# A vision tower on one core: the context from the normalised tokens times the keys, convolutions straight to tokens, a 128+64 split of 192 rows, and a new order on every engine

## The chip, the cores and the metric

The kernel runs on 1 core of one Trainium2 chip. Its time is the device time of one launch in microseconds (us). The kernel before takes 154.59 us, the median of 3 runs (153.43, 154.59, 155.02). Five engines work side by side, each through its own list of instructions in order: TensorE (PE in the rows; its weight loads are PEld), VectorE (DVE), ScalarE (ACT), GpSimd (POOL) and SyncE (SP), which issues the DMAs. They wait for each other by semaphores.

## What is computed

Two images of 32x128x128 are cut into 256 patches of 8x8 each. A convolution turns a patch into a token of 128 numbers. Two layers follow, then a head to 192 numbers per token, a linear attention and a feed-forward of 768 hidden units. Cut to what matters:

```
x = patches @ conv_w + conv_b
for each of 2 layers:
    y = ln(x) * g + b
    q, k, v = split(y @ qkv_w)                  # 8 heads of 64
    q = softmax(q, over a head's 64) * scale
    k = softmax(k, over the 256 tokens)
    x = x + (q @ (k^T v)) @ out_w + out_b
    x = x + gelu((ln(x)*g2+b2) @ ff1_w + ff1_b) @ ff2_w + ff2_b
h = ln(x) @ head_w + head_b                     # 192 wide
q, k, v = split(layernorm(h) @ W_qkv)           # 12 heads of 16
q, k = elu(q) + 1, elu(k) + 1
h = h + ((q @ (k^T v)) / (q . sum(k) + eps)) @ W_out + b_out
h = h + new_gelu(layernorm(h) @ W0 + b0) @ W1 + b1
```

## The kernel before

Everything is float32. A token tile is 128 tokens, so an image has two (`TILES`). Products that feed softmax or gelu are made from three products of reduced precision: operand a is split into `a_hi` (rounded) and `a_lo = a - a_hi`, and hi*hi, lo*hi and hi*lo are added in PSUM (`split_product`, L302, used by `weight_left` and `weight_right`). Those matmuls are one instruction each in the trace. A float32 matmul or product with plain operands shows as two MATMUL instructions.

**First stage.** SyncE issues all loads in one queue; `conv` (L320) adds 16 chunks of 128 channels-times-pixels for image 0 and 16 for image 1, with the convolution weight as the stationary operand and 256 tokens as the moving one. The result stands with the 128 features on the partitions, so ScalarE adds the bias (`embedding_bias`) and TensorE transposes it (L328) before VectorE can take the statistics of a token.

**Second stage, four steps.** A step `s` is one attention of one image: layer `s // 2`, image `s % 2`. The loop over `STEPS` sets the order on each engine: keys and queries of the step (`qkv_k`, `qkv_q`), values (`qkv_v`), transposed keys (`turn_k`, L379), `context` (L389: values times keys, eight 128x128 products of float32), `turn_q`, `context_out` (L398), `attend` (L413, which gives x after attention). Between them stands the feed-forward of the step before (`ff1`, `ff2`, L437) for the other image. In step 0 the place of the feed-forward is taken by the last 8 of the 16 chunks of image 1's convolution.

A layer norm (LN) is a chain over three engines: VectorE takes statistics (L645, L648) and adds epsilon (L650), GpSimd raises to the power -1/2 (`rsqrt`, tile `rstd`, L1103), VectorE subtracts and scales (`norm_apply`, tile `xn`, L655), TensorE transposes (L336), VectorE writes the high part with gain and offset (`norm_out_hi`, L662), ScalarE the exact value (L955), and VectorE or GpSimd their difference (`norm_out_lo`). GpSimd also makes the low parts of the weights (`weight_low_part`, L1157), adds bias rows, scales q, and multiplies the mixing masks into the last weights (`mix_fc` L1143, `mix_proj` L1150).

**Last stage.** After the fourth attention come, for each image, the remaining feed-forward, the last LN, `head`, LN3, `qkv3`, the linear attention, LN4, `fc3` and `proj3` (L561). The 192 rows of these products are cut in two chunks of 96, so a product takes 3 x 2 = 6 matmuls. Image 0's last products fill the gaps of image 1's attention. The raw weights of layer 1 and of the last products lie where `embed_sb` was, so their loads wait for the end of both convolutions.

## Time and profile before

| | |
|---|---|
| runs | 155.02, 154.59, 153.43 us; median 154.59 |
| profiled execution | span 154.1 us from its first to its last instruction; no other time is given for it |
| TensorE busy | 131.1 us, 85% |
| VectorE, ScalarE, GpSimd busy | 93.7, 66.0, 49.1 us |
| first key product | starts at 23.4 us |
| fourth attention added to x | at 95.3 us |
| last output instruction | starts at 151.25 us |

The profile is of one execution. Its span lies 0.5 us below the median of the three runs. The busy time of TensorE counts overlapping ends once; two matmuls of the same form that follow each other without a gap show their pace by the distance of their starts, or by the length of a group divided by its count.

### The profile page before, as it was taken

To read this page: it belongs to the slowest core of one execution; us is meant where nothing else is said; L and a number is where in the kernel's file an instruction comes from. 1 tells how busy PE (TensorE), PEld (TensorE's weight loads), DVE (VectorE), ACT (ScalarE), POOL (GpSimd) and SP (SyncE) were. 2 spreads that over 40 slices of the span, in tenths; PEclk is the share of its full clock that TensorE was granted. 3 is DMA by queue.
4 is the path that set the end of the run, shared out by engine and by line. 5 is a ranking of instruction groups with operands and counts; after the bars stand their busy time and mean duration, and the time that the engine had idled before them with its cause. 6 is when DMAs were issued, how large, how long until landed. Compare 5 with 4: busy or idle time off the path is not lost.

```text
span 154.1 us, 2173 instructions
## 1 busy us (share of the span) xinstructions
PE 131.1 (85%) x790; PEld 113.1 (73%) x790; DVE 93.7 (61%) x236; ACT 66.0 (43%) x149; POOL 49.1 (32%) x60
## 2 busy tenths in 40 slices
PE   1699889999779989799797996769987959999993
PEld 1468668797658968589576984559876948999992
DVE  1200087947799668977689757773957796145201
ACT  3010313906559746697375981144222040163230
POOL 0000020074162953447553673180671060004000
PEclk9999999999999999999999999956977995599999
DMA  5999997008800000000000000000000000000101
GB/s 161 285 421 415 421 412 262 0 4 265 209 0 0 6 0 0 0 0 4 0 0 0 0 4 0 0 0 2 2 0 0 4 0 0 0 4 0 51 0 51
DMA packets 3388, 11.50 MB, mean 75 GB/s; under 512 B 393, under 2 KB 1385, under 8 KB 3122
## 3 DMA queue, kind: packets, MB, share of 16 engines
q1 hardware_dynamic: 3378, 11.37, 20.6%
q8 instruction: 6, 0.10, 0.2%
q14 instruction: 4, 0.03, 0.1%
HBM read 10.98 MB, written 0.39 MB: 74 GB/s over the span
## 4 chain that ended last, share of the span: by engine, by line
PE 55%; DVE 26%; issue 5%; POOL 5%; ACT 3%; DMA 3%; SPq 0%; DVEq 0%; ACTq 0%; POOLq 0%
PE bank L302 16%; DVE xn L655 10%; PE bank L320 10%; PE bank L437 5%; PE bank L389 5%; PE bank L561 5%; POOL rstd L1103 3%; DMA embed_sb<-in_embed 3%; DVE stats L645 2%; DVE yT_hi L662 2%; DVE nkmax L695 2%; POOL yT_lo L1109 1%; PE bank L336 1%; PE bank L531 1%; PE bank L339 1%
## 5 line engine op out<-in xcount | busy, mean ns | idle before, releaser
L1103 POOL TENSOR_TENSOR rstd<-var,minus_half 128x2 f32<-128x2 f32 x14 | 10.2, 726 | 69.8 <-DVE var L650 69.8
L655 DVE TENSOR_SCALAR xn<-x,mv,rstd 128x128 f32<-128x128 f32 x20 | 13.8, 732 | 4.2 <-POOL rstd L1103 4.2
L320 PE MATMUL bank<-embed_sb 128*128 128x256 f32 x32 | 12.0, 544 | 4.4 <-DMA embed_sb<-in_embed 4.4
L955 ACT ACTIVATE yT<-bank,small_sb 128x256 f32<-128x256 f32 x10 | 5.7, 565 | 19.5 <-DVE yT_hi L662 16.4
L320 PEld LDWEIGHTS bank<-embed_sb 128*128 128x128 f32 x32 | 8.5, 277 | 7.2 <-DMA embed_sb<-in_embed 5.1
L1122 POOL TENSOR_TENSOR qn<-q,rqsum 128x512 f32<-128x512 f32 x8 | 8.2, 1044 | 15.2 <-DVE rqsum L719 15.2
L336 PE MATMUL bank<-small_sb,xn 128*128 128x128 f32 x20 | 4.4, 301 | 7.6 <-DVE xn L655 7.6
L413 PE MATMUL bank<-cw,qT 128*128 128x128 f32 x64 | 10.0, 289 | 0.4
L413 PEld LDWEIGHTS bank<-cw,qT 128*128 128x128 f32 x64 | 8.2, 190 | 2.0 <-issue 1.3
L336 PEld LDWEIGHTS bank<-small_sb,xn 128*128 128x128 f32 x20 | 2.0, 141 | 10.3 <-DVE xn L655 10.3
L975 ACT ACTIVATE kexp<-bank,nkmax 128x256 f32<-128x256 f32 x16 | 7.4, 473 | 4.3 <-DVE nkmax L695 4.3
L437 PE MATMUL bank<-restw,hid 128*128 128x128 f32 x64 | 9.1, 302 | 0.0
L437 PEld LDWEIGHTS bank<-restw,hid 128*128 128x128 f32 x64 | 8.8, 219 | 0.0
L389 PE MATMUL bank<-ktok,vtok 128*128 128x128 f32 x64 | 8.0, 278 | 0.4
L689 DVE COPY x<-bank 128x256 f32<-128x256 f32 x2 | 0.8, 420 | 12.3 <-PE bank L328 12.3
L561 PE MATMUL bank<-projw_raw,patches_sb 128*128 128x192 f32 x48 | 8.3, 326 | 0.0
L389 PEld LDWEIGHTS bank<-ktok,vtok 128*128 128x128 f32 x64 | 7.5, 192 | 1.0 <-issue 0.9
L655 DVE TENSOR_SCALAR xn<-h,mv,rstd 128x192 f32<-128x192 f32 x8 | 6.5, 859 | 2.2 <-POOL rstd L1103 2.2
L561 PEld LDWEIGHTS bank<-projw_raw,patches_sb 128*128 128x128 f32 x48 | 7.7, 190 | 0.0
L320 PE MATMUL bank<-patches_sb,embed_sb 128*128 128x256 f32 x32 | 7.6, 379 | 0.0
L302 PE MATMUL bank<-qkvw_hi,yT_hi 128*128 128x512 f32 x16 | 6.8, 427 | 0.8 <-DVE yT_hi L662 0.8
L1007 ACT ACTIVATE hid<-bank,small_sb 128x256 f32<-128x256 f32 x16 | 6.4, 474 | 2.0 <-PE bank L302 1.9
(142 smaller groups left out, 349.1 us busy)
## 6 DMA issues: line engine op xcount, KB each, us to landing
embed_sb<-in_embed SPq DMA_DIRECT2D x3, 768.0 KB, 7.9
patches_sb<-in_patches SPq DMA_DIRECT2D x2, 1024.0 KB, 12.1
restw<-in_rest_w SPq DMA_DIRECT2D x2, 768.0 KB, 16.1
qkvw<-in_qkv_w SPq DMA_DIRECT2D x3, 256.0 KB, 11.0
embed_sb<-in_qkv_w SPq DMA_DIRECT2D x1, 768.0 KB, 4.7
embed_sb<-in_embed SPq DMA_DIRECT2D x1, 576.0 KB, 4.4
projw_raw<-in_proj_w SPq DMA_DIRECT2D x1, 576.0 KB, 16.2
embed_sb<-in_fc_w SPq DMA_DIRECT2D x1, 576.0 KB, 7.6
```

The costliest lines, as they stand in the source:

```text
L302: mm = nc.tensor.matmul(dst, left(a, n), right(b, n), start=(k == 0 and n == 0), stop=(last and n == chunks - 1))
L320: mm = nc.tensor.matmul(dst[:, 0:TOKENS], embed_sb[:, c, 0:D], rhs, start=(c == 0), stop=(c == KCONV - 1))
L336: mm = nc.tensor.transpose(dst[:, t * P:(t + 1) * P], xn[i][:, t, 0:D], ident)
L389: mm = nc.tensor.matmul(VB[0][:, p * P:(p + 1) * P], vtok[i][:, t, p * P:(p + 1) * P], ktok[i][:, t, p * P:(p + 1) * P], start=(t == 0), s ...
L413: mm = nc.tensor.matmul(VB[0][:, t * D:(t + 1) * D], qT[i][:, t, c * P:(c + 1) * P], cw[i][:, c, :], start=(c == 0), stop=(c == PAIRS - 1))
L437: mm = nc.tensor.matmul(banks[t][:, 0:D], hid[i][:, c, t * P:(t + 1) * P], ff2w(l, c), start=(c == 0), stop=(c == FC - 1))
L561: mm = nc.tensor.matmul(QB[t][:, 0:E], hid3[i][:, c, t * P:(t + 1) * P], projw[:, c, :], start=(c == 0), stop=(c == HC - 1))
L655: last = nc.vector.tensor_scalar(xn[i][:, t, 0:width], src[:, t, 0:width], mv[i][:, t, 0:1], rstd[i][:, t:t + 1], ALU.subtract, ALU.mult)
L975: nc.scalar.activation(kexp[i][:, c, :], KB[c // 2][:, (c % 2) * TOKENS:(c % 2 + 1) * TOKENS], ACT.Exp, bias=nkmax[i][:, c:c + 1], accum_o ...
L1007: nc.scalar.activation(hid[i][:, c, :], src[:, (c % 2) * TOKENS:(c % 2 + 1) * TOKENS], ACT.Gelu, bias=col("ff1_b", l * FC + c)).then_inc(h ...
L1103: nc.gpsimd.tensor_tensor(rstd[i][:], var[i][:], minus_half[:], ALU.pow).then_inc(rstd_ready[i], 1)
L1122: nc.gpsimd.tensor_tensor(qn[i][:, t, :].rearrange("p (h d) -> p h d", h=HEADS), q[i][:, t, :].rearrange("p (h d) -> p h d", h=HEADS), rqs ...
```

## The change

Five things are changed at once.

1. **Context without v.** `qkv_v` and its two evictions are gone. The context k^T v = (k^T y) W_v is made from `keys_of_y`: two float32 products of 512 columns (y of a token tile against the keys of that tile), one eviction `ykey` in two halves (VectorE, then ScalarE), and four 128x128 products with the raw value weights. For that y must stand with tokens on the partitions, so LN1 is finished there: VectorE's `centre_and_gain` (x minus mean, times gain row) and `scale_and_offset` (times 1/deviation, plus offset row) replace `norm_apply`; after the transpose ScalarE copies the high part and VectorE subtracts it for the low part. Gain and offset rows come by two new broadcast loads. Epsilon is folded into the statistics, so L650 is gone.
2. **Token convolutions.** The token tile is stationary and the convolution weight moves: two products of 128 columns per chunk in place of one of 256, the bias as one more product (`conv_bias`), and no transposes. `warm_up` products of constants (8 calls) stand ahead of and between the first chunks.
3. **128+64 rows.** The 192 rows are cut into 128 and 64. High and low part of the 64 stand in one operand of 128 rows (`yT3_rest`), so a product takes 5 matmuls instead of 6.
4. **The last attention** multiplies q by the masked context first (`numerators3`, 102 columns per half: 96 of context and 6 of key sums), divides, then transposes and multiplies by the output weight. The product with ones over the tokens is gone.
5. **Order.** The loops are gone. Each engine's list is written out instruction by instruction, with PSUM banks given step by step; the weights no longer share memory with `embed_sb`, so no load waits.

```diff
         def _(sp):
-            half = KCONV // 2
-            for j in range(CONV_PIECES):
-                at = slice(CONV_AT[j], CONV_AT[j + 1])
-                sp.dma_start(embed_sb[:, at, :], embed0[:, at, :]).then_inc(loaded[f"embed{j}"], 16)
-                if j == 1:
-                    sp.dma_start(mix_sb[:], mix).then_inc(loaded["mix"], 16)
-                    sp.dma_start(small_sb[:], small).then_inc(loaded["small"], 16)
...
-            for i in range(IMAGES):
-                for t in range(TILES):
-                    sp.wait_ge(outs_ready[i], t + 1)
...
+            load_embed(0, 1, "embed0")
+            load_embed(1, 4, "embed1")
+            load_embed(8, 12, "embed3")
+            load_embed(12, 16, "embed4")
+            load_embed(4, 8, "embed2")
+            load(convb_sb[:], convb, "cb")
+            load_patches(0, 8, "patches1a")
+            load(qkvw[0][:, INNER:2 * INNER], qkv_w[0][:, INNER:2 * INNER], "qkv0k")
+            load(qkvw[0][:, 0:INNER], qkv_w[0][:, 0:INNER], "qkv0q")
+            load_patches(8, 16, "patches1b")
...
+            load(rows_sb[:], rows.to_broadcast([P, NROW]), "rows")
+            load(aqkvw[:], aqkv_w, "aqkv")
...
+            load(headw[:], head_w, "head")
+            load(qkvw[0][:, 2 * INNER:], qkv_w[0][:, 2 * INNER:], "v0")
+            load(qkvw[1][:], qkv_w[1], "qkv1")
+            load(restw[0][:], rest_w[0], "rest0")
+            load(mix_sb[:], mix, "mix")
+            load(projw[:], proj_w, "proj")
+            load(fcw[:], fc_w, "fc")
+            sp.wait_ge(out_ready, 2)
...
+            def warm_up(dst, n):
+
+                for _ in range(n):
+                    mm = nc.tensor.matmul(dst[:, 0:E], ones[:, 0:P], ones[:], start=True, stop=True)
                 return mm
...
-            def conv(i, dst, first=0, last=KCONV):
+            def conv(i, first, last):
 
                 for c in range(first, last):
-                    if i == 0 and c in CONV_AT:
-                        pe.wait_ge(loaded[f"embed{CONV_AT.index(c)}"], 16)
-                    if i == 1 and c % (KCONV // 2) == 0:
-                        pe.wait_ge(loaded["patches1a" if c == 0 else "patches1b"], 16)
...
-                    mm.then_inc(conv_done, 1)
-
-            def embedding_to_tokens(i, dst):
-                pe.wait_ge(embT_ready[i], 1)
+                    for t in range(TILES):
+                        left = (embed_sb[:, c, D + t * P:D + (t + 1) * P] if i == 0
+                                else patches1_sb[:, c, t * P:(t + 1) * P])
+                        mm = nc.tensor.matmul(CONV_BANK[i][t][:, 0:D], left, embed_sb[:, c, 0:D],
+                                              start=(c == 0), stop=False)
+                return mm
+
+            def conv_bias(i, t):
+                return nc.tensor.matmul(CONV_BANK[i][t][:, 0:D], ones[:, 0:P], convb_sb[:], start=False, stop=True)
+
...
+            def keys_of_y(s, t):
+
+                return nc.tensor.matmul(YK_BANK[s][:], y[s % IMAGES][:, t, :], ktok[:, t, :],
+                                        start=(t == 0), stop=(t == TILES - 1))
+
+            def context(s, half):
+
+                for p in (2 * half, 2 * half + 1):
+                    at = 2 * INNER + p * P
+                    mm = nc.tensor.matmul(CTX_BANK[s][:, p * P:(p + 1) * P], qkvw[s // IMAGES][:, at:at + P],
+                                          ykey[:, p * P:(p + 1) * P], start=True, stop=True)
+                return mm
+
...
-            def qkv_v(l, i, t):
-
-                if t == 0:
-                    pe.wait_ge(split_lo[f"qkv{l}"], 3)
-                    if l or i:
-                        pe.wait_ge(x_mid[1 - i], l + i)
-                weight_right(VB[t][:], lambda part, n: (yT_hi, yT_lo)[part][i][:, t * P:(t + 1) * P],
-                             lambda part, n: qkvw_parts[l][part][:, 2 * INNER:3 * INNER],
-                             (yT_lo_ready[i], LN1(l) + 1)).then_inc(v_done[i], 1)
...
+            def rows192(dst, i, t, at, stages):
+
+
+                tile = slice(t * P, (t + 1) * P)
+                if "high" in stages:
+                    nc.tensor.matmul(dst, yT3_hi[i][:, tile], aqkvw_parts[0][:, 0, at], start=True, stop=False)
+                    mm = nc.tensor.matmul(dst, yT3_hi[i][:, tile], aqkvw_parts[1][:, 0, at], start=False, stop=False)
+                if "low" in stages:
+                    nc.tensor.matmul(dst, yT3_lo[i][:, tile], aqkvw_parts[0][:, 0, at], start=False, stop=False)
+                    nc.tensor.matmul(dst, yT3_rest[i][:, tile], aqkvw_parts[0][:, 1, at], start=False, stop=False)
+                    mm = nc.tensor.matmul(dst, yT3_rest[i][:, tile], aqkvw_parts[1][:, 1, at], start=False, stop=True)
+                return mm
+
...
+            def numerators3(i):
+                for t in range(TILES):
+                    for c in range(ECH):
+                        at = (t * ECH + c) * KVW
+                        mm = nc.tensor.matmul(NUM3_BANK[i][:, at:at + KVW], qT3[i][:, c, t * P:(t + 1) * P],
+                                              kv3[i][:, c, :], start=True, stop=True)
+                return mm
...
+            def fc3(i, c):
+                at = slice(c * P, (c + 1) * P)
+                dst = FC3_BANK[i][c // 2][:, (c % 2) * TOKENS:(c % 2 + 1) * TOKENS]
+                nc.tensor.matmul(dst, fcw_parts[0][:, 0, at], yT3_hi[i][:], start=True, stop=False)
+                nc.tensor.matmul(dst, fcw_parts[1][:, 0, at], yT3_hi[i][:], start=False, stop=False)
+                nc.tensor.matmul(dst, fcw_parts[0][:, 0, at], yT3_lo[i][:], start=False, stop=False)
+                nc.tensor.matmul(dst, fcw_parts[0][:, 1, at], yT3_rest[i][:], start=False, stop=False)
+                return nc.tensor.matmul(dst, fcw_parts[1][:, 1, at], yT3_rest[i][:], start=False, stop=True)
+
...
+            def mean_and_variance(i, t, of):
+                return nc.vector.bn_aggr(mv[i][:, t, :], of[i][:, t, :])
+
+            def centre_and_gain(s, t):
+                l, i = divmod(s, IMAGES)
+                return nc.vector.scalar_tensor_tensor(out=xg[i][:, t, :], in0=x[i][:, t, :], scalar=mv[i][:, t, 0:1],
+                                                      in1=norm_rows_sb[l][:, 0:D], op0=ALU.subtract, op1=ALU.mult)
+
+            def scale_and_offset(s, t):
+                l, i = divmod(s, IMAGES)
+                return nc.vector.scalar_tensor_tensor(out=y[i][:, t, :], in0=xg[i][:, t, :], scalar=rstd[i][:, t:t + 1],
+                                                      in1=norm_rows_sb[l][:, D:2 * D], op0=ALU.mult, op1=ALU.add)
...
+            qk_low_part(1, 1)
+            low_part(aqkvw_parts[1][:, 0, :], aqkvw[:, 0, :], aqkvw_parts[0][:, 0, :])
+            pool.wait_ge(mean1_ready, 6)
+            inverse_deviation(0).then_inc(deviation1_ready, 1)
+            pool.wait_ge(mean2_ready, 4)
+            inverse_deviation(1).then_inc(deviation2_ready, 1)
+            pool.wait_ge(ff_in_ready, 2)
+            low_part(yT_lo[1][:], yT[1][:], yT_hi[1][:]).then_inc(ff_in_low, 1)
+            low_part(ff1w_parts[1][1][:], ff1w(1), ff1w_parts[1][0][:])
+            add_row(0, bias_row("out_b", 1)).then_inc(x_and_out_bias, 1)
+            pool.wait_ge(loaded["fc"], 16)
+            mix_fc(0).then_inc(fc_mixed, 1)
+            add_row(1, bias_row("ff2_b", 0)).then_inc(x_and_ff2_bias, 1)
+            pool.wait_ge(mean1_ready, 8)
+            inverse_deviation(1).then_inc(deviation1_ready, 1)
+            mix_fc(1).then_inc(fc_mixed, 1)
+            pool.wait_ge(q_inverse_ready, 5)
+            normalise_q(2, 0).then_inc(q_normalised, 1)
```

**TensorE, first stage.** `embed_sb` and `patches_sb` are operands of the convolutions of image 0 and 1, `small_sb` is the identity of a transpose. Before, from the first chunk to the first query product:

```order
L320 MATMUL bank<-embed_sb 128x256 x4
L446 MATMUL bank<-mix_sb,alpha_mask_e 96x16 x2
L448 MATMUL bank<-mix_sb,alpha 128x192
L320 MATMUL bank<-embed_sb 128x256 x12
L328 MATMUL bank<-small_sb,embT 128x128 x2
L320 MATMUL bank<-patches_sb,embed_sb 128x256 x6
L336 MATMUL bank<-small_sb,xn 128x128 x2
L320 MATMUL bank<-patches_sb,embed_sb 128x256 x2
L302 MATMUL bank<-qkvw_hi,yT_hi 128x512
```

Now, from the second warm-up (products of `ones`) to the first key product:

```order
L309 MATMUL bank<-ones 128x192 x2
L318 MATMUL bank<-embed_sb 128x128 x18
L309 MATMUL bank<-ones 128x192 x2
L318 MATMUL bank<-embed_sb 128x128 x12
L318 MATMUL bank<-embed_sb,patches_sb 128x128 x8
L323 MATMUL bank<-convb_sb,ones 128x128
L318 MATMUL bank<-embed_sb,patches_sb 128x128 x4
L323 MATMUL bank<-convb_sb,ones 128x128
L318 MATMUL bank<-embed_sb,patches_sb 128x128 x16
L327 MATMUL bank<-small_sb,y 128x128 x2
L318 MATMUL bank<-embed_sb,patches_sb 128x128 x4
L351 MATMUL bank<-yT_hi,qkw_hi 128x256
```

Image 1's convolution is complete, but for its bias, before the first key product; before, half of it was left.

**TensorE, step 0, around the context.** `kexp`, `ktok` are the keys before and after the transpose. Before:

```order
L379 MATMUL bank<-small_sb,kexp 128x128 x8
L320 MATMUL bank<-patches_sb,embed_sb 128x256 x4
L389 MATMUL bank<-ktok,vtok 128x128 x8
L320 MATMUL bank<-patches_sb,embed_sb 128x256 x4
L405 MATMUL bank<-small_sb,qn 128x128 x4
L328 MATMUL bank<-small_sb,embT 128x128 x2
```

Now, from the first product of y with the keys to the context:

```order
L374 MATMUL bank<-ktok,y 128x512
L351 MATMUL bank<-yT_hi,qkw_hi 128x256
L351 MATMUL bank<-yT_hi,qkw_lo 128x256
L374 MATMUL bank<-ktok,y 128x512
L358 MATMUL bank<-yT_lo,qkw_hi 128x256
L339 MATMUL bank<-qkw_hi,yT_hi 128x512
L339 MATMUL bank<-qkw_lo,yT_hi 128x512
L381 MATMUL bank<-ykey,qkvw 128x128 x4
```

The eight context products have become two of 512 columns and four of 128, and the other image's keys and queries (L339, L351, L358) stand between them where a convolution stood.

**GpSimd, around the norms of steps 2 and 3.** `rstd` is the power of a norm. Before:

```order
L1103 TENSOR_TENSOR rstd<-var,minus_half 128x2
L1143 TENSOR_TENSOR embed_sb<-embed_sb,fc_mix 96x768
L1103 TENSOR_TENSOR rstd<-var,minus_half 128x2
L1117 TENSOR_TENSOR xb<-x,rows_sb 128x256
L1157 TENSOR_TENSOR aqkvw_lo<-embed_sb,aqkvw_hi 96x576
L1109 TENSOR_TENSOR yT_lo<-yT,yT_hi 128x256
L1122 TENSOR_TENSOR qn<-q,rqsum 128x512 x2
L1117 TENSOR_TENSOR xb<-x,rows_sb 128x256
L1157 TENSOR_TENSOR aqkvw_lo<-embed_sb,aqkvw_hi 96x576
L1103 TENSOR_TENSOR rstd<-var,minus_half 128x2
```

Now, from the norms at the start of step 2 to the scaling of its q:

```order
L1756 TENSOR_TENSOR rstd<-mv,minus_half 128x2 x2
L1759 TENSOR_TENSOR yT_lo<-yT,yT_hi 128x256
L1759 TENSOR_TENSOR ff1w_lo<-restw,ff1w_hi 128x512
L1766 TENSOR_TENSOR xb<-x,rows_sb 128x256
L1785 TENSOR_TENSOR fcw<-fcw,fc_mix 128x768
L1766 TENSOR_TENSOR xb<-x,rows_sb 128x256
L1756 TENSOR_TENSOR rstd<-mv,minus_half 128x2
L1785 TENSOR_TENSOR fcw<-fcw,fc_mix 128x768
L1774 TENSOR_TENSOR qn<-q,rqsum 128x512 x2
```

Before, a long instruction on weights (`embed_sb`, `fcw`, `aqkvw`) follows a `rstd` without a wait. Now the second row of two `rstd` is followed by `yT_lo`, which waits for the very norm it belongs to; one `rstd` is still followed by `fcw`.

## Rows read from the trace of the kernel before

**Rows 1.** The page: busy time of the engines; GB/s in 40 slices.
```profile
PE 131.1 (85%) x790; PEld 113.1 (73%) x790; DVE 93.7 (61%) x236; ACT 66.0 (43%) x149; POOL 49.1 (32%) x60
GB/s 161 285 421 415 421 412 262 0 4 265 209 0 0 6 0 0 0 0 4 0 0 0 0 4 0 0 0 2 2 0 0 4 0 0 0 4 0 51 0 51
```

**Rows 2.** Windows: length, busy (x) of PE, PEld, DVE, ACT, POOL; granted clock, DMA.
```profile
0.00:23.45 23.45, 17.63 (x58) 12.89 (x59) 5.42 (x19) 3.77 (x8) 1.19 (x5) 1.00 0.93 353
23.45:40.43 16.98, 15.74 (x102) 13.44 (x101) 12.05 (x27) 7.74 (x22) 4.67 (x5) 1.00 0.44 141
58.51:76.79 18.28, 15.82 (x112) 13.77 (x113) 14.81 (x36) 12.45 (x28) 9.66 (x10) 1.00 0.00 1
76.79:95.30 18.51, 15.82 (x112) 13.73 (x112) 14.59 (x35) 13.26 (x29) 10.08 (x10) 1.00 0.00 1
95.30:151.25 55.95, 50.04 (x296) 45.54 (x296) 31.60 (x87) 16.56 (x37) 14.25 (x20) 0.85 0.01 4
```

**Rows 3.** Chain of waits, 71 to 77 us: start, length, engine and what.
```profile
71.58 0.50 DVE x L753 x2
73.09 0.71 POOL rstd L1103
73.83 1.75 DVE xn L655 x2
76.79 0.47 PE bank L302
```

**Rows 4.** Timeline (start, length), the page's group of xn, and tile xn (min/median/max ns).
```profile
20.34 0.68 DVE L685 TENSOR_TENSOR qkvw_lo<-qkvw,qkvw_hi 128x512 fp32r<-128x512 f32 x1
20.61 0.98 POOL L1103 TENSOR_TENSOR rstd<-var,minus_half 128x2 f32<-128x2 f32 x1 [20.17 <-DVE var L650]
21.63 0.60 DVE L655 TENSOR_SCALAR xn<-x,mv,rstd 128x128 f32<-128x128 f32 x2 [0.60 <-POOL rstd L1103]
73.76 1.47 POOL L1143 TENSOR_TENSOR embed_sb<-embed_sb,fc_mix 96x768 f32<-96x768 f32 x1
L655 DVE TENSOR_SCALAR xn<-x,mv,rstd 128x128 f32<-128x128 f32 x20 | 13.8, 732 | 4.2 <-POOL rstd L1103 4.2
L655 DVE TENSOR_SCALAR xn<-x,mv,rstd x20: 332/344/1816, 21.6 to 110.9; 128x128 f32<-128x128 f32 x20
```

**Rows 5.** Timeline, TensorE: start, length from first start to last end.
```profile
11.53 1.91 PE L320 MATMUL bank<-embed_sb 128*128 128x256 f32 x4
32.52 1.89 PE L320 MATMUL bank<-patches_sb,embed_sb 128*128 128x256 f32 x8
60.22 0.28 PE L302 MATMUL bank<-yT_hi,qkvw_hi 128*128 128x256 f32 x1
60.34 0.28 PE L302 MATMUL bank<-yT_hi,qkvw_lo 128*128 128x256 f32 x1
61.64 0.40 PE L302 MATMUL bank<-qkvw_lo,yT_hi 128*128 128x512 f32 x1
61.87 0.40 PE L302 MATMUL bank<-qkvw_hi,yT_lo 128*128 128x512 f32 x1
67.28 2.02 PE L389 MATMUL bank<-ktok,vtok 128*128 128x128 f32 x16
147.40 4.07 PE L561 MATMUL bank<-projw_raw,patches_sb 128*128 128x192 f32 x24
```

**Rows 6.** Windows: three stretches of the last stage.
```profile
98.00:100.00 2.00, 1.05 (x5) 0.64 (x6) 1.44 (x7) 0.68 (x2) 0.00 (x0) 1.00 0.00 0
100.40:107.40 7.00, 5.84 (x27) 5.51 (x28) 3.77 (x6) 3.34 (x6) 3.06 (x3) 0.52 0.00 1
127.00:134.30 7.30, 7.30 (x33) 6.38 (x33) 3.20 (x9) 0.22 (x1) 0.00 (x0) 0.54 0.00 0
```

**Rows 7.** Timeline, VectorE: a three-operand instruction, and the last two.
```profile
111.17 1.01 DVE L773 SCALAR_TENSOR_TENSOR ktok<-bank,kexp 128x384 f32<-128x384 f32 x2
151.25 0.62 DVE L824 TENSOR_TENSOR outs<-bank,hb 128x192 f32<-128x192 f32 x2 [7.53 <-PE bank L561]
```

2384 lines of the change are left out of this document (1519 added, 865 removed).

## The prediction

> **What bounds the kernel now.** I read the busy times first: TensorE is busy 85% of the span, VectorE 61% [rows 1]. Then the windows, cut at three moments: the first key product (23.45 us), the fourth attention added to x (95.30) and the last output instruction (151.25) [rows 2]. They give three stages of 23.5, 71.9 and 58.8 us (the last with what follows 151.25). Then the pace of TensorE's instructions [rows 5], to tell work from waiting; then the chain of waits inside one step [rows 3].
>
> The pace at the full clock of 2.4 GHz: 0.12 us for a reduced product of 256 columns (60.22 to 60.34) and 0.23 for one of 512. A float32 product is two instructions, each 0.123 for 128 columns (2.02 us by 16; a product 0.246), 0.165 for 192, 0.23 for 256 [rows 5]. Transposes take one instruction of about 0.12. At the start the same 256 columns take 0.43 each (1.91 us less the last one's overlap, 4 instructions): that is the 1.2 GHz level, although the windows write 1.00 for the granted clock there [rows 2, 5].
>
> Stage two holds four attentions and three feed-forwards. An attention is, in instructions: transposes of y 0.24, keys 12 x 0.12 = 1.44, q 6 x 0.23 = 1.38, v 1.38, key transposes 0.96, context 8 x 0.246 = 1.97, q transposes 0.96, context_out 0.98, attend 1.97: 11.3 us. A feed-forward is 0.24 + 1.44 + 1.97 = 3.65. With half a convolution (8 x 0.46 = 3.7) and its transposes this is 60.1 us of work in 71.9 us, 84%. The other 11.8 us are waits, and the chain shows the dearest: in each step the LN1 of the other image runs through VectorE and GpSimd with little left for TensorE [rows 3]. Inside it, two `xn` take 1.75 us where they took 0.60 at 21.63: the first starts at 73.83, while GpSimd multiplies weights from 73.76 for 1.47 us, and ends with it [rows 3, 4]. All 20 `xn` from x cost 13.8 us; at their minimum of 0.33 they would cost 6.6 [rows 4].
>
> Stage three is a longer chain with thinner cover: TensorE is busy 50 of 56 us, but much of that at the low clock. After two us with TensorE half busy (98 to 100) the granted clock falls to 0.52 for 7 us, and again in 127 to 134.3 [rows 6].
>
> **The change part by part.**
>
> *Stage one.* The work is 2 x 0.246 = 0.49 us per chunk against 0.46: 1 us more over both images, plus four bias products (1.0) and eight warm-ups; it saves two transposes and two ScalarE evictions. The warm-ups start after the memset, at about 1.1 us: eight instructions of 192 columns at the low level, 0.32 each by the 0.43, or 2.6 us. The chunks come at about 415 GB/s once the queue runs [rows 1]: 3.15 MB for image 0 by about 11 us, image 1's second half by about 18, the identity by about 18.5. From 3.7 us I lay down 64 instructions for image 0, 56 for image 1 and the biases at 0.123, with low-clock pace for the first few and waits for the loads to about 12 us. The transpose of y comes at about 22.5 and the first key product at 23.6 us. Before: 23.45. No gain in time, but 3.7 us of convolution no longer lie in stage two. If the low pace lasts until 14 us as now, stage one is 2 us longer; if loads and clock are better, 2 shorter. Stage one: **23.6**.
>
> *Stage two, work.* v goes (1.38). Context was 1.97 and is now two products of 512 columns and four of 128. No row has float32 at 512 columns; bounds are 0.23 (the 256-column instruction) and 0.92 (four times it) for each of four instructions. I take 0.46, since 128 and 256 columns scale nearly with the columns: 1.84 + 0.98. An attention becomes 10.75, 0.5 less. Four of them, three feed-forwards and the mixing masks (18 small instructions, 2.2) make 56.2 us.
>
> *Stage two, waits.* Two things shrink them. The other image's keys and queries now stand between the transposes, the products with y and the context, so both images' chains run side by side, and y of image 1 is ready some 3 us after the first key. And GpSimd's order: of the places where a `rstd` is followed without a wait by a long weight instruction, one or two remain, so most of the 7.2 us of excess in `xn` goes. Against it: LN1 has four VectorE instructions instead of two. A three-operand one of 384 columns takes 0.54 [rows 7]; one of 128 I put at 0.3 (bounds 0.28, from the slope of 384 to 128 columns, and 1.8, the blocked maximum of rows 4). `centre_and_gain` runs during the power, so 0 to 0.6 of it shows. VectorE's work per step stays near 14 us (14.8 busy in a step now, blocked time included [rows 2]), so neither engine has room for a step under 14.5. I walked step 0 and 1 through the new lists with these durations: x after attention of image 0 at 40.9 us, of image 1 at 53.3, where before they stood at 40.4 and 58.5. TensorE then works 90% and more of the time. For the whole stage I take 90%: 56.2 / 0.90 = **62.4**, so it ends at 86.0 against 95.3. The bounds are 84% as now (66.9) and 95% (59.2).
>
> GpSimd's power itself took 0.98 us at 20.61, where it takes 0.71 otherwise, with VectorE's two-input `qkvw_lo` running until 21.02 [rows 3, 4]. The Trainium skill says the same of its cause (SBUF — State Buffer, section Who interferes with whom): VectorE with two inputs in SBUF and GpSimd reading SBUF lock each other out for a whole instruction. By that rule `centre_and_gain`, which has two such inputs where `xn` has one, holds up the power it should hide behind, and `scale_and_offset` can be held up in turn. That speaks against finishing y on the token side; by it each of four LN1 would lose up to 0.3 us, and the sum would be 1.2 more.
>
> *Stage three.* Work: head 1.3, transposes 2.3, feed-forward 3.4, `qk3` and v 5.7 (40 matmuls for 48), context, q and numerators 5.5, attend 2.6, `fc3` 60 x 0.12 = 7.2 (for 72: 8.6), `proj3` 24 x 0.33 = 7.9: 36 us for about 40. The chain of image 1, walked the same way from its x after attention: LN2 and first feed-forward input 4.3, feed-forward done at 12.5, last LN turned 16.3, head 17.6, LN3 turned 21.8, split 23.8, `qk3` and v 27.2 (image 0's attend between), numerators done 31.6, divided 33, turned and attended 36.6, LN4 turned 40.4, split 41.7, `fc3` and `proj3` 8.1, output and its DMA 2.9 (151.25 to 154.1 [rows 7]): 52.7, less 1.3 because VectorE's pairs overlap. The numerators put two more hand-overs into the chain; turning `att3` and evicting it costs what turning q did before. So **51.4** against 58.8. The floor is 46 (work plus the norms nothing covers), the ceiling 58.
>
> *Sum.* 23.6 + 62.4 + 51.4 = 137.4 us for the span, against its own 154.1. The median of the runs lies 0.5 above that profile, within their spread of 1.6, so I forecast **137.5 us**.
>
> **The rivals.**
>
> *The last stage keeps its low clock and its waits.* The new stage three also has thin stretches (36 us of work in 51), and rows 6 show what one costs. If the 14 us of rows 6 again run at 1.2 GHz, up to 7 us come back, and with stage two at 84% 4.5 more: 142 to 149. For it: the numerators' chain. Against: image 0's products are spread over image 1's waits. Chance 0.20.
>
> *TensorE and VectorE both run nearly full.* Stage two at 95%, stage three at 46 to 48, the sum is 128 to 132. For it: the written order overlaps at single instructions, where the loop overlapped at blocks. Chance 0.12.
>
> *Slower: the convolutions never leave 1.2 GHz long enough, and the lists inherit it.* The place is the load-paced first stage, with waits for five pieces. The price is half a us for each us spent at the low level in which TensorE is the bound. It decides from 34 us at the low level on, beyond what my walk has (17 us to recover); all of stage three's work and half of stage two's at 1.2 GHz give 137 + 18 to 36, or 155 to 173. Against it: TensorE works without a break from the first chunks on, and steps as dense as these hold 1.00 now [rows 2]. Chance 0.05.
>
> *The change doesn't do what it says: VectorE takes over as the bound.* If its 14.8 busy us a step were work and not blocked time, with the two added instructions a step would be 16 to 18 us, and with stage three unchanged the time 152 to 156. Chance 0.04.
>
> **How the numbers follow.** The forecast (133 to 142) has 0.59. About 1% (1.5 us) is what a measurement of this kernel can tell from no change. The two likely rivals on either side reach the range of 130 to 146, which leaves out the lower part of the second, the upper part of the first, and the last two: about 0.18. Faster 0.92, same 0.03, slower 0.05.
>
> **What would show it.** Right: the first key product at 22 to 26 us with image 1's convolution done; 256-column steps of image 0's chunks at the fast pace before 10 us; x after the fourth attention at 82 to 90; `xn` and `y` at a median near 0.35 with one or two blocked; from there 48 to 55 us to the end. Wrong: a product of y and keys far from 0.9 us; stage two under 84% with waits of TensorE for `y` or `ykey`; long stretches of stage three near 0.5. The forecast would fail most easily in stage three, where my walk gives every hand-over its minimum.

## The result, and the profile after

Four runs of the changed kernel took 136.95, 137.02, 137.91 and 138.37 us, median **137.47**; four of the kernel before took 153.25 to 155.02, median 154.01. The ratio is 0.891, with a 95% interval of 0.884 to 0.898. The forecast was 137.5. The profiled execution is the one of 136.95 us; its span is 135.2, so 1.75 us lie outside the span. (Medians are over all runs; ratios and intervals leave disturbed runs out.)

The page of the changed kernel: the busy times, then TensorE's busy tenths and its granted clock in 40 equal slices.

```profile
span 135.2 us, 2174 instructions
...
PE 119.6 (88%) x818; PEld 104.0 (77%) x818; DVE 77.6 (57%) x241; ACT 61.9 (46%) x147; POOL 48.7 (36%) x60
...
PE   6859999899999998985999999479987789999992
...
PEclk9999999999999999999999999977999999999999
```

Against [rows 1] TensorE is busy 11.5 us less and the span is 18.9 shorter, 2.4 more than the medians are apart: the profile of before is of a long execution, as the part on the prediction works out. VectorE fell by 16.1 us, from 93.7 to 77.6, although it has five instructions more; that is the largest fall of any engine. The clock row is 9 everywhere but in two slices.

The same three stages as in [rows 2], cut at the first key product (22.79), at the start of the last addition of the fourth attention to x (83.21) and at the end. Columns: stretch, its length, busy time and instructions of the engines, granted clock, DMA share, GB/s.

```profile
0.00:22.79 22.79, 19.67 (x151) 19.20 (x151) 5.54 (x26) 3.38 (x6) 1.18 (x5) 1.00 0.90 345
22.79:83.21 60.42, 56.83 (x385) 46.41 (x383) 45.75 (x126) 38.98 (x102) 32.66 (x35) 1.00 0.16 64
83.21:135.20 51.99, 43.05 (x287) 38.41 (x286) 26.27 (x90) 19.53 (x40) 14.83 (x20) 0.97 0.03 9
```

Stage one takes 22.8 us (before 23.5), stage two 60.4 (71.9), stage three 52.0 (58.8). In stage two TensorE is busy 56.8 of 60.4 us, or 94%. The prediction worked out 84% for before, 60.1 of 71.9, from paces. Measured as here, before has 63.2 us and 88% in the same stretch:

```profile
23.45:95.30 71.85, 63.19 (x437) 54.70 (x436) 56.05 (x131) 45.66 (x106) 33.67 (x35) 1.00 0.13 39
```

So the stage lost 6.4 us of TensorE's work and 5.1 us of its waits.

The normalised tiles, for which [rows 4] show those made from x before: minimum, median and maximum of each instruction in ns. The first line is of the kernel before, for the tiles made from h; the others are of the changed kernel.

```profile
L655 DVE TENSOR_SCALAR xn<-h,mv,rstd x8: 368/896/1871, 101.0 to 140.9; 128x192 f32<-128x192 f32 x8
...
L942 DVE TENSOR_SCALAR xn<-x,mv,rstd x12: 325/344/843, 40.8 to 99.3; 128x128 f32<-128x128 f32 x12
...
L942 DVE TENSOR_SCALAR xn<-h,mv,rstd x8: 374/378/380, 93.8 to 122.3; 128x192 f32<-128x192 f32 x8
...
L938 DVE SCALAR_TENSOR_TENSOR y<-xg,rstd,norm_rows_sb x8: 338/348/1552, 20.9 to 62.9; 128x128 f32<-128x128 f32 x8
```

The medians lie close to the minima now. The eight `xn` from h cost VectorE 6.5 us before and cost 2.7 now. Two blocked pairs are left, and the timeline shows the dearer one (start, duration, engine, line, what; in brackets the idle time before):

```profile
60.65 0.73 POOL L1756 TENSOR_TENSOR rstd<-mv,minus_half 128x2 f32<-128x2 f32 x1 [1.29 <-DVE mv L929]
...
61.36 1.47 POOL L1785 TENSOR_TENSOR fcw<-fcw,fc_mix 128x768 f32<-128x768 f32 x1
...
61.42 1.81 DVE L938 SCALAR_TENSOR_TENSOR y<-xg,rstd,norm_rows_sb 128x128 f32<-128x128 f32 x2 [0.33 <-POOL rstd L1756]
...
63.29 0.33 PE L327 MATMUL bank<-small_sb,y 128*128 128x128 f32 x1 [0.75 <-DVE y L938]
```

GpSimd multiplies weights (`mix_fc`) from 61.36 to 62.83, and the two `y` of step 3 take 1.81 us for 0.61; the transposes of y wait 0.75 us on TensorE. The other is a pair of `xn` of 1.10 us at 87.46, beside GpSimd's `yT_lo`.

The last thin place, in windows of 2 us (same columns):

```profile
86.00:88.00 2.00, 0.28 (x2) 0.28 (x2) 1.61 (x8) 0.56 (x1) 0.94 (x2) 1.00 0.01 4
88.00:90.00 2.00, 1.07 (x6) 0.67 (x6) 0.56 (x1) 0.56 (x1) 1.17 (x2) 0.92 0.02 4
90.00:92.00 2.00, 2.00 (x8) 2.00 (x8) 0.61 (x3) 0.00 (x0) 0.00 (x0) 0.50 0.00 0
92.00:94.00 2.00, 2.00 (x13) 1.78 (x13) 0.97 (x6) 0.95 (x3) 1.67 (x2) 0.73 0.00 0
```

TensorE is busy 0.28 of 2 us, then 1.07 of 2, and the granted clock falls to 0.50, the 1.2 GHz level, until 93 us. Before, it had fallen three times, for 7, 4 and 7 us [rows 6 show two of them]; here once, for 3.5.

### The profile page after: what moved, and what is told of

Read it like the earlier page. It is cut to its first block, busy times and chain, and to the rows that moved or that the text cites. A ratio compares the mean times of both kernels' runs of the same rounds, so it can differ in the third digit from the quotient of the medians.

```text
span 135.2 us, 2174 instructions
## 1 busy us (share of the span) xinstructions
PE 119.6 (88%) x818; PEld 104.0 (77%) x818; DVE 77.6 (57%) x241; ACT 61.9 (46%) x147; POOL 48.7 (36%) x60
## 4 chain that ended last, share of the span: by engine, by line
PE 53%; DVE 25%; ACT 8%; DMA 6%; POOL 3%; issue 3%; SPq 1%
PE bank L318 9%; DMA embed_sb<-in_embed 6%; PE bank L494 5%; PE bank L412 4%; PE bank L374 3%; PE bank L400 3%; POOL rstd L1756 3%; DVE xn L942 3%; PE bank L327 2%; PE bank L351 2%; PE bank L430 2%; DVE nkmax L959 2%; DVE q L971 2%; DVE stats L923 2%; DVE y L938 2%
## 5 line engine op out<-in xcount | busy, mean ns | idle before, releaser
L1756 POOL TENSOR_TENSOR rstd<-mv,minus_half 128x2 f32<-128x2 f32 x14 | 10.1, 721 | 45.6 <-DVE mv L929 45.6
L318 PE MATMUL bank<-embed_sb 128*128 128x128 f32 x64 | 8.4, 283 | 2.0 <-DMA embed_sb<-in_embed 2.0
L494 PE MATMUL bank<-projw,patches_sb 128*128 128x192 f32 x48 | 8.9, 328 | 0.0
L374 PE MATMUL bank<-ktok,y 128*128 128x512 f32 x16 | 8.2, 605 | 0.2 <-DVE ktok L985 0.2
L494 PEld LDWEIGHTS bank<-projw,patches_sb 128*128 128x128 f32 x48 | 7.7, 189 | 0.3 <-ACT patches_sb L1542 0.3
L318 PE MATMUL bank<-embed_sb,patches_sb 128*128 128x128 f32 x64 | 7.8, 275 | 0.0
L318 PEld LDWEIGHTS bank<-embed_sb,patches_sb 128*128 128x128 f32 x64 | 7.5, 192 | 0.0
L400 PE MATMUL bank<-yT_hi,ff1w_hi 128*128 128x256 f32 x16 | 5.6, 358 | 1.9 <-ACT yT L1503 1.9
L967 DVE TENSOR_REDUCE nqmax<-bank 128x8 f32<-128x512 f32 x8 | 5.4, 677 | 2.7 <-PE bank L345 2.7
L364 PE MATMUL bank<-small_sb,kexp 128*128 128x128 f32 x32 | 5.7, 281 | 0.5 <-ACT kexp L1507 0.5
```

The costliest lines, as they stand in the source:

```text
L318: mm = nc.tensor.matmul(CONV_BANK[i][t][:, 0:D], left, embed_sb[:, c, 0:D], start=(c == 0), stop=False)
L364: mm = nc.tensor.transpose(KT_BANK[s][t][:, c * P:(c + 1) * P], kexp[:, c, t * P:(t + 1) * P], ident)
L374: return nc.tensor.matmul(YK_BANK[s][:], y[s % IMAGES][:, t, :], ktok[:, t, :], start=(t == 0), stop=(t == TILES - 1))
L400: mm = nc.tensor.matmul(FF1_BANK[s][c // 2][:, (c % 2) * TOKENS:(c % 2 + 1) * TOKENS], ff1w_parts[l][part][:, c * P:(c + 1) * P], yT_hi[i][:],
L494: return nc.tensor.matmul(PROJ3_BANK[i][t][:, 0:E], hid3[i][:, c, t * P:(t + 1) * P], projw[:, c, :], start=(c == 0), stop=(c == HC - 1))
L967: return nc.vector.tensor_reduce(nqmax[s % IMAGES][:, t, :], by_head(Q_BANK[s][t][:]), AX_X, ALU.max, negate=True)
```

## The experiments

Twelve kernels ran. Those whose label begins with b are edits of the kernel before, those with a of the changed kernel. All edits of one group shared a chip and its runs of the kernel before, whose median was 153.62, 155.18 and 154.66 us in the three groups; the ratios are to those. The changed kernel was not run again in these groups, so a difference from its 137.47 us is one between chips. A kernel's runs differ by 1 to 3.5%, in part as the mean granted clock of the run differs. Where a difference of 1 us matters I therefore also use the profiled span from the first key product to the end, which for the changed kernel is 135.2 - 22.79 = 112.4 us. It is of one execution each; the four spans of the changed kernel alone lie 1.4 us apart.

I call it a lock when a VectorE and a GpSimd instruction overlap and one of them takes longer than it does alone, by up to the whole of the other.

### GpSimd's order, in the kernel before

```diff
@@ gpsimd, for s in range(STEPS) @@
+    norm_out_lo(ip, LN2(lp))          # ahead of add_bias and the low parts of this step
...
-    rsqrt(1 - i, LN1((s + 1) // 2))   # stood ahead of the step's long weight instruction
     if s == 1: qkv1_low_part(2)
     if s == 2: mix_fc(1)
     if s == 3: weight_low_part("fc", 1, ...)
     if s == 0: weight_low_part("ff1_0", 1, ...)
+    rsqrt(1 - i, LN1((s + 1) // 2))
```

(The second low part of fc went behind `mix_proj`, one `add_bias3` ahead of a power.)

> The kernel before, with GpSimd's order alone changed: the long weight instructions (low parts and mixing products, 1.3 to 1.8 us each) stand ahead of the power of the LN1, or behind yT_lo, so that none follows a power whose normalisation VectorE is about to do. Theory A, the one of the forecast: seven pairs of xn took 1.54 to 2.07 us where 0.60 is their minimum, because GpSimd multiplied weights beside them; all xn from x fall from 13.8 us to under 8, and of the 7 us of excess the LN1 half (4.5 us) lies on the chain, so the time is 147 to 151. Rival B: TensorE's order of blocks bounds the step and the excess was cover, or the long instructions block whatever VectorE does at their new place: 153 to 155.

Measured: 144.06 us (142.16 to 147.16), ratio 0.942, interval 0.906 to 0.977. Nothing but the order of one engine was changed, and by the medians it gives 9.6 of the 16.5 us; by the interval at least 3.6. Its page, its `xn` from x, and its last two stages, cut at 22.10 and 87.96:

```profile
PE 125.1 (88%) x790; PEld 108.6 (76%) x790; DVE 86.6 (61%) x236; ACT 66.0 (46%) x149; POOL 49.1 (34%) x60
...
PEclk9999999999999999999999999757999999999999
```

```profile
L655 DVE TENSOR_SCALAR xn<-x,mv,rstd x20: 334/342/586, 20.3 to 102.0; 128x128 f32<-128x128 f32 x20
...
22.10:87.96 65.86, 62.72 (x437) 54.65 (x436) 49.77 (x130) 45.59 (x106) 33.66 (x35) 1.00 0.16 51
87.96:142.60 54.64, 45.77 (x296) 41.78 (x296) 31.44 (x88) 16.54 (x37) 14.22 (x20) 0.93 0.03 8
```

The 20 `xn` have a median of 0.342 and a maximum of 0.586 us where the kernel before had 1.816. VectorE is busy 86.6 us for 93.7. That these 7.1 us match the excess that the prediction worked out from [rows 4] (7.2) is chance: they are a balance. By VectorE's busy time in each group of instructions, the `xn` from x fell by 7.6 us (13.8 to 6.2) and those from h by 1.4 (6.5 to 5.1), while the additions of epsilon (`var`) rose by 1.3 (2.4 to 3.7) and those to the denominators (`den`) by 0.9 (0.3 to 1.2). At their new places the long instructions block these:

```profile
83.74 1.80 POOL L1157 TENSOR_TENSOR fcw_lo<-embed_sb,fcw_hi 96x768 fp32r<-96x768 f32 x1
84.58 0.98 DVE L650 TENSOR_SCALAR var<-mv 128x2 f32<-128x2 f32 x1
...
105.59 1.81 POOL L1157 TENSOR_TENSOR fcw_lo<-embed_sb,fcw_hi 96x768 fp32r<-96x768 f32 x1
106.36 1.07 DVE L790 TENSOR_SCALAR den<-den 128x24 f32<-128x24 f32 x1
```

An addition to 2 columns takes 0.98 us for 0.17 and ends with GpSimd's subtraction. Other VectorE work beside the long instructions kept its length: the sums over q (`qsum`, read from SBUF) 0.68 us, the additions to x, with one input in PSUM, 0.49 a pair. Stage two takes 65.9 us for 71.9, stage three 54.6 for 58.8. TensorE's work there is nearly the same (62.7 us for 63.2), so its waits fell from 8.7 to 3.1 us. The span fell by 11.5. Of this 1.4 us lie in stage one, which the edit leaves alone; the other 10.2 are still more than the 7.1: the granted clock is low in one stretch of 7 us (91 to 98) instead of three. Theory A in its mechanism, and 3 us more than its range; of its rival, the blocking at the new places is there too, at 2.2 us.

### The filled waits, in the kernel before

```diff
+    def fill(dst, n):                 # products of ones, 192 columns, never read
+        for _ in range(n): nc.tensor.matmul(dst[:, 0:E], ones[:, 0:P], ones[:], start=True, stop=True)
...
+    fill(CB, 3)      # ahead of turn_norm(0, LNF)
+    fill(CB, 2)      # ahead of ff1(1, 1)
+    fill(QB[0], 3)   # ahead of turn_norm(0, LN3)
+    fill(KB[1], 1)   # behind turn_norm(1, LNF)
+    fill(CB, 4)      # ahead of turn_norm(0, LN4)
+    fill(KB[1], 1)   # behind it
```

> The kernel before, with 14 float32 products of ones (192 columns, results never read) laid into five waits of TensorE between 92 and 126 us. Theory A: the granted clock falls after TensorE has waited, and rows before show it low in 100.4 to 107.4, 113 to 117 and 126.6 to 134.3 us; with the waits filled it stays at 1.00, 19 us at half speed become at best 9.5, and since TensorE is the bound in perhaps two thirds of them the time falls by 3 to 7 us, to 147 to 151. Rival B: the clock falls whatever TensorE does there, or the chain of this stage goes through VectorE and GpSimd, so that a faster TensorE only waits longer: 153 to 155, and the filler itself may cost up to 1.

Measured: 149.51 us (147.66 to 151.20), ratio 0.975, interval 0.945 to 1.004. The interval touches no change. Of its four runs three had a mean granted clock of 1.00 (147.66, 148.28, 150.75); the kernel before never had more than 0.965 in its 29 runs beside the experiments. The medians say 4 us, inside theory A; the size is not settled.

### Both together, in the kernel before

The edits of the last two experiments.

> The kernel before with GpSimd's order and the filled waits, and its own place of the convolution. GpSimd's order alone gave 144.1 (9.5 us less) and left 4.6 us of missing clock (91 to 98 and at the end); the waits filled alone gave 149.5 (4 less). Theory A, two separate causes: 140 to 142.5, the sum less what the shorter waits already saved of the clock. Rival B, one cause (shorter waits keep the clock up by themselves): 143.5 to 145, no better than the order alone.

Measured: 146.93 us (143.88 to 147.11), ratio 0.947, interval 0.921 to 0.972: no better than the order alone. Its clock row:

```profile
PEclk9999999999999999999999999789995599999999
```

The stretch at 91 to 98 us is shorter, but a new one of 7 us stands at 109 to 116, where TensorE waits again and no filler lies. Nearer to rival B: once GpSimd's order is changed, no gain of the filler is seen here (ratio 0.947 for 0.942, with intervals that overlap).

### Image 1's convolution first, in the kernel before

```diff
-    turn_norm(0, LN1(0), CB)
-    conv(1, SB_, 6, 8)
+    conv(1, SB_, 6, KCONV)
+    turn_norm(0, LN1(0), CB)
...                                    # and no conv(1, ...) in step 0
```

> The kernel before, with all of image 1's convolution written ahead of the first transpose and key product (half of it stood in the first step). Theory A: TensorE waits for loads in stage one and has room there, the first key product comes at most 1 us later than 23.45, and 3.7 us of work leave a stage two in which TensorE is busy 84%: 150 to 152. Rival B: image 1's second half is loaded only at about 18 us and its 3.7 us of products delay the first key product by 2 to 4 us, while in step 0 they filled waits that now stay empty: 153 to 157.

Measured: 156.32 us (154.10 to 158.84), ratio 1.018, interval 0.986 to 1.050. TensorE around the first key product:

```profile
9.84 7.86 PE L320 MATMUL bank<-embed_sb 128*128 128x256 f32 x24
...
18.67 7.07 PE L320 MATMUL bank<-patches_sb,embed_sb 128*128 128x256 f32 x32
...
26.69 0.47 PE L302 MATMUL bank<-qkvw_hi,yT_hi 128*128 128x512 f32 x1 [0.73 <-DVE yT_hi L658]
```

The key product starts 3.2 us later than in [rows 2], and the time from there to the fourth attention shrinks only from 71.9 to 70.3 us. That the convolution leaves stage two is worth 1.6 us there and costs 3.2 in front: rival B by the profile, while the interval of the runs allows no loss too. In the changed kernel, where the first key product comes at 22.8, the transposes of y are written between chunk 14 and the last two, and image 0's chunks end at 15.2 us for 17.9; these are the likely reasons that it costs nothing there, not tried one by one.

### All three, in the kernel before

The three edits above.

> The kernel before with all three edits: GpSimd's order, the filled waits, the convolution first. Nothing of v, of the token-side LN, of the 128 and 64 rows or of the order of TensorE, VectorE and ScalarE is taken over. If the three effects are separate they add up, 8 to 14 us in all: 140 to 146. If the written order itself (both images' chains side by side) carries the gain, the three give under 6 us: 148 to 152, and the changed kernel's 137.5 is due to what is missing here.

Measured: 146.51 us (146.08 to 147.68), ratio 0.966, interval 0.951 to 0.981. By the medians that is close to the order of GpSimd less what the moved convolution costs. The effects don't add to 140. Whether the gain is under the 6 us of the second theory stays open: it is 7.1 us by the medians and 5.2 by the ratio. Its first key product comes at 25.25 us. Stage two has waits of 4.2 us; about 1.0 of the busy 60.3 is filler:

```profile
25.25:89.71 64.46, 60.28 (x426) 52.65 (x426) 49.80 (x130) 45.48 (x106) 33.62 (x35) 1.00 0.11 32
```

### The changed kernel with the locks put back

```diff
@@ gpsimd @@
     inverse_deviation(0).then_inc(deviation2_ready, 1)        # LN2, step 0
+    qk_low_part(1, 1)
...
     inverse_deviation(1).then_inc(deviation2_ready, 1)        # LN2, step 1
+    low_part(aqkvw_parts[1][:, 0, :], ...)
...
     inverse_deviation(1).then_inc(deviation2_ready, 1)        # LN2, step 3
+    low_part(fcw_parts[1][:, 0, :], ...)                      # each taken away from its former place
```

> The changed kernel with three long GpSimd weight instructions (1.27, 1.40 and 1.83 us) put right behind a power, as the kernel before had them: behind the LN2 power of step 0, of step 1 and of step 3. Theory A: each holds up the normalisation that VectorE does then, by 1.0 to 1.5 us, and since TensorE and VectorE are both nearly full, most of it shows: 140 to 142. Rival B: the written order has other work to put in TensorE's way while VectorE waits, so a lock costs little here: 137.5 to 139.

Measured: 143.01 us (142.42 to 144.38), ratio 0.942, interval 0.930 to 0.954: 5.5 us more than the changed kernel by the medians, 7.9 by the ratios, above the upper end of theory A. The pair of step 1, and the clock row:

```profile
53.42 0.69 POOL L1756 TENSOR_TENSOR rstd<-mv,minus_half 128x2 f32<-128x2 f32 x1 [0.19 <-DVE mv L929]
...
54.08 1.39 POOL L1759 TENSOR_TENSOR aqkvw_lo<-aqkvw,aqkvw_hi 128x576 fp32r<-128x576 f32 x1
...
54.15 1.67 DVE L942 TENSOR_SCALAR xn<-x,mv,rstd 128x128 f32<-128x128 f32 x2
...
55.88 0.33 PE L327 MATMUL bank<-small_sb,xn 128*128 128x128 f32 x1 [1.29 <-DVE xn L942]
```

```profile
PE 123.3 (88%) x818; PEld 108.1 (77%) x818; DVE 80.9 (57%) x241; ACT 61.9 (44%) x147; POOL 48.6 (35%) x60
...
PEclk9999999999997799689999999995999999999999
```

The three pairs of `xn` take 1.50, 1.67 and 2.07 us for 0.60 each, and VectorE is busy 80.9 us for 77.6: 3.3 us of locks. The rest goes with the clock: all six runs have a mean of 0.952 or 0.964, the changed kernel's 0.975 or 0.987, and TensorE is busy 123.3 us for 119.6 with the same 818 instructions. TensorE waits 1.29 us for that `xn` at 55.88, and the granted clock is low at 44 to 47, 58 to 61 and 95 to 99 us, where the changed kernel's profile has one such stretch. A lock costs its own length and, in these six runs, some clock behind it.

### One GpSimd product moved, in the changed kernel

```diff
     pool.wait_ge(mean1_ready, 8)
     inverse_deviation(1).then_inc(deviation1_ready, 1)
-    mix_fc(1).then_inc(fc_mixed, 1)
...
     normalise_q(2, 1).then_inc(q_normalised, 1)
+    mix_fc(1).then_inc(fc_mixed, 1)
```

> The changed kernel with one long GpSimd product (mix_fc of the second chunk, 1.47 us) moved from right behind the power of step 3's LN1 to behind the normalisation of q of step 2. Theory A: the pair y of step 3 falls from 1.81 to 0.61 us; the wait of TensorE behind it (0.75 us before the turn at 63.29) goes and the end comes 0.7 to 1.2 us sooner: 136.3 to 136.8. Rival B: VectorE's k, q work of step 2 behind it is the bound anyway, or the product blocks something else at its new place: 137.2 to 138.

Measured: 136.14 us (134.53 to 137.92), ratio 0.880, interval 0.871 to 0.890. The two `y` take 0.61 us at 62.82; key product to end is 134.6 - 23.42 = 111.2 us for 112.4. So 1.2 us from the span and 1.3 from the medians, though the interval overlaps that of the changed kernel.

The profile's 1.2 us don't lie where the edit is. From the key product to the last addition of the fourth attention (at 83.66) it takes 60.2 us for 60.4, although the granted clock is low from 54 to 57; from there to the end it takes 50.9 for 52.0, because this profile has no low stretch in the last stage. Inside stage two the pair `y` comes 39.4 us after the key product for 38.6, behind the low stretch, so about 1.0 us was won after it. That is the size of theory A, but the total is not shown by this experiment.

### The clock held up, in the changed kernel

```diff
     turn(TURN2_BANK[3], xn[1]).then_inc(xn_turned, 1)
+    warm_up(bank[6], 5)
     pe.wait_ge(ff_in_ready, 4)
     ff1_high(3, 0)
+    warm_up(bank[6], 1)
...
+    warm_up(bank[6], 1)
     pe.wait_ge(head_in_ready, 1)
```

> The changed kernel with seven products of ones (192 columns) laid into the waits of TensorE at 86.0 to 87.7 (1.75 us), 88.2 (0.39) and 89.2 (0.54). Theory A: these waits are what brings the clock down to 0.50 in 89.5 to 93.4; filled, it stays at 1.00 and TensorE's 3.6 us there become 1.9; the chain goes through them, so the end comes 1 to 1.8 us sooner: 135.7 to 136.5. Rival B: the low stretch only moves to the next thin place (102 to 106 us), or VectorE's chain takes over: 137 to 138.

Measured: 136.46 us (135.40 to 137.00), ratio 0.885, interval 0.878 to 0.892. TensorE at the head, before and after the edit:

```profile
89.71 1.65 PE L430 MATMUL bank<-headw,yT 128*128 128x192 f32 x4 [0.54 <-ACT yT L1503]
```

```profile
86.94 1.79 PE L309 MATMUL bank<-ones 128*128 128x192 f32 x10
...
90.85 0.92 PE L430 MATMUL bank<-headw,yT 128*128 128x192 f32 x4 [0.21 <-ACT yT L1506]
...
PEclk9999999999999999599999999999999999999999
```

The four instructions of the head take 0.92 us for 1.65. But they do so without the filler too. The profile of the kernel with `mix_fc` moved has the same three waits as the changed kernel (1.75, 0.39 and 0.54 us) and its clock stays at 1.00:

```profile
88.17 0.39 PE L400 MATMUL bank<-yT_hi,ff1w_hi 128*128 128x256 f32 x1 [1.75 <-ACT yT L1503]
...
90.16 0.92 PE L430 MATMUL bank<-headw,yT 128*128 128x192 f32 x4 [0.54 <-ACT yT L1503]
```

So does the kernel with y and keys doubled. That the filler held the clock up is therefore not shown by this place. The last stage takes 50.9 us with the filler and 50.9 in that unfilled profile, for 52.0 in the changed kernel: its low stretch cost about 1 us, and the filler bought nothing beyond its absence. This profile has a low stretch at 54 to 57 us instead, and from the key product to the end it takes 112.3 us for 112.4. Three of the six runs have a mean clock of 0.998 (135.40, 135.62, 136.48), which none of the changed kernel's four has; three have 0.987 like its best (136.43, 136.83, 137.00). The median lies in theory A's range, 1.0 us under the changed kernel's, with intervals that overlap: not settled.

### Both, and `yT_lo` on VectorE

```diff
@@ vector, behind normalise(0, 1, x, D) of the last LN @@
+    dve.wait_ge(ff_in_ready, 4)
+    low_part(yT_lo[1][:], yT[1][:], yT_hi[1][:]).then_inc(ff_in_low, 1)
```

(together with the two edits above; GpSimd's own `yT_lo` of that step is gone)

> The changed kernel with mix_fc of the second chunk moved (136.14 alone), the waits at 86 to 89 us filled (136.46 alone), and yT_lo of the last feed-forward made by VectorE behind the last LN's normalisation instead of by GpSimd beside it. If the effects add: 134.5 to 135.3. If the clock only falls in another place, or VectorE's added 0.5 us stands in the way: 135.8 to 136.8.

Measured: 136.18 us (135.55 to 137.44), ratio 0.897, interval 0.885 to 0.909. The span is the shortest of the profiled ones with 133.8, but from the key product 111.4, no better than the moved product alone. One reason stands in its timeline:

```profile
86.61 0.69 POOL L1761 TENSOR_TENSOR rstd<-mv,minus_half 128x2 f32<-128x2 f32 x1 [1.89 <-DVE mv L932]
...
87.26 0.73 POOL L1771 TENSOR_TENSOR xb<-x,rows_sb 128x256 f32<-128x256 f32 x1
87.33 0.99 DVE L945 TENSOR_SCALAR xn<-x,mv,rstd 128x128 f32<-128x128 f32 x2 [0.38 <-POOL rstd L1761]
```

With `yT_lo` gone, GpSimd's next instruction, an addition of a bias row, moved up behind the power and blocks the same `xn` (0.99 us for 1.10). The second theory's range. The three small edits together gain nothing over one of them: 136.1, 136.5 and 136.2 us lie within each other's spread, no run here has a mean clock above 0.987 in spite of the filler, and the ratio is no lower than the changed kernel's 0.891.

### Without the warm-ups

```diff
-    warm_up(bank[1], 4)      # and both warm_up(bank[1], 2)
```

> The changed kernel (137.47) without the eight products of ones in the first 12 us. Theory A, the forecast's: stage one is paced by the loads and ends within 1 us of 22.8 whether the first chunks run at the low or the high clock, so 137 to 138.5. Rival B: without the warm-ups the low level of 1.2 GHz lasts through image 0's chunks (64 instructions at 0.23 for 0.12) and the work spills over the loads: the first key product 2 to 3 us later, 139.5 to 141.

Measured: 138.61 us (137.66 to 140.03), ratio 0.899, interval 0.890 to 0.909. The first key product comes at 24.26 us instead of 22.4 to 23.4 in the other versions of the changed kernel. The second group of chunks, of this kernel and of the changed one:

```profile
5.35 2.07 PE L318 MATMUL bank<-embed_sb 128*128 128x128 f32 x8 [0.62 <-DMA embed_sb<-in_embed]
```

```profile
1.12 2.93 PE L309 MATMUL bank<-ones 128*128 128x192 f32 x8 [1.12 <-DVE stats L1069]
...
5.18 1.05 PE L318 MATMUL bank<-embed_sb 128*128 128x128 f32 x8
```

Eight instructions take 2.07 us without and 1.05 with the products of ones. Image 0's chunks end at 16.7 us for 15.2, and these 1.5 us get through to the key product, so the loads alone do not pace stage one. Between the two theories; by the medians the warm-ups are worth about 1 us, with intervals that overlap.

### One product of y and keys twice

```diff
+    if t == 0:
+        nc.tensor.matmul(YK_BANK[s][:], y[s % IMAGES][:, t, :], ktok[:, t, :], start=True, stop=True)
     return nc.tensor.matmul(YK_BANK[s][:], y[s % IMAGES][:, t, :], ktok[:, t, :], ...)
```

> The changed kernel with the first product of y and the exponentiated keys of each step done twice (four extra float32 products of 512 columns, 0.92 us each by its trace, 3.7 us in all; the first result is overwritten). It prices one us of TensorE's work in stage two. Theory A: TensorE works 94% of stage two, so nearly all shows: 140.4 to 141.2, slope 0.8 to 1. Rival B: VectorE's chain bounds the steps and half of it hides: 138.5 to 139.8.

Measured: 140.78 us (139.84 to 142.08), ratio 0.917, interval 0.909 to 0.924: 3.3 us more for 3.7 us of work, and 115.4 us from the key product for 112.4. One us of TensorE's work in stage two costs 0.8 to 0.9 us of time. Theory A.

### Six products for five

```diff
+    nc.tensor.matmul(dst, fcw_parts[0][:, 0, at], yT3_hi[i][:], start=True, stop=True)
     nc.tensor.matmul(dst, fcw_parts[0][:, 0, at], yT3_hi[i][:], start=True, stop=False)
...                                    # likewise the first product in rows192
```

> The changed kernel with a sixth reduced product in every group of five for q, k and v of the last attention and for fc3 (the first product done twice), as many as 96 and 96 rows need: 12 of 256 columns at 0.12, 4 of 384 at 0.175, 4 of 192 at 0.11 by its trace, 2.6 us in all. Theory A: fc3 and the products stand on TensorE's own path in stage three, so 2 to 2.7 us come on top: 139.5 to 140.2. Rival B: the waits of stage three (TensorE busy 83%) take up those of q, k and v: 138.3 to 139.3.

Measured: 139.57 us (138.29 to 140.16), ratio 0.918, interval 0.909 to 0.927: 2.1 us more; from the key product 114.1 for 112.4. The last stage has it (columns as above):

```profile
82.88:136.50 53.62, 45.30 (x307) 40.95 (x306) 26.27 (x90) 19.55 (x40) 14.75 (x20) 0.97 0.03 8
```

Stage three takes 53.6 us for 52.0, and TensorE is busy 45.3 for 43.05. The sixth product, which the split into 128 and 64 rows saves, is worth 1.6 to 2.1 of its 2.6 us. Theory A, at its lower end.

## Why the prediction was right

**The result stands on errors of opposite sign, and that it is met to 0.03 us is luck.** The forecast of 137.5 was the sum for the span, 137.4. The spans of the four runs were 135.2, 135.2, 136.1 and 136.6, so the sum was 0.8 to 2.2 us too large; and 1.8 us lie outside the span in every run, which the sum left out because the profile of before showed no own time. It should have been said as an unknown. With these 1.8 us the profile of before would be of an execution of about 155.9 us, above all its four runs, and not 0.5 us below their median.

**Stage one, 23.6; measured 22.8.** The first key product at 22.79 lies in the range named (22 to 26), image 1's convolution is done but for the two bias products, and the chunks run at 0.13 us from 5.18 us on. The price put on the low pace at the start, 2 us, was sized well: 1.5 without the warm-ups.

**The price of y and keys, 0.46 per instruction between 0.23 and 0.92.** The trace has it:

```profile
30.40 0.95 PE bank L374 x2
...
31.59 0.88 PE bank L374 x2
...
L374 PE MATMUL bank<-ktok,y x16: 591/592/697, 30.2 to 75.4; 128*128 128x512 f32 x16
```

Two instructions take 0.88 to 0.95 us on the chain. That is proportional to the columns, as taken. (The 592 ns of the group's own row count the overlap of each with the next.)

**Stage two, work 56.2 and 90%.** TensorE is busy 56.8 us, and 94% of the stage; the 62.4 was 2.0 too long, inside its bounds. The 84% of before, from which the share was raised, is 88% by the windows: its work was put 3.1 us too low. The walk was late by a similar share: x after attention of image 0 at 39.33 for 40.9, of image 1 at 50.85 for 53.3. The share was chosen between 84 and 95 with no row to decide it. That was the weakest number in the sum and it erred by the most.

**Where the waits went.** The prediction named two causes, the written order and GpSimd's. It did not say how much each is. The profiles do, for stage two, as length, TensorE's busy time and its waits in us: before 71.9, 63.2, 8.7; with GpSimd's order alone 65.9, 62.7, 3.1; with all three edits 64.5, 60.3 (about 1.0 of it filler), 4.2; changed 60.4, 56.8, 3.6. So GpSimd's order alone, in the old loop, takes away as much waiting as the whole change. What the changed kernel has beyond it in this stage is less work, 5.9 us, of which 3.7 are the convolution and about 2 are v (an estimate, 0.5 us an attention; v was not tried alone). For the whole kernel GpSimd's order is 9.6 of the 16.5 us by the medians, and put back in part it costs 5.5. That includes the granted clock, which the prediction counted under stage three and did not tie to the locks.

The rest, between the profiles of GpSimd's order alone (142.6) and the changed kernel (135.2), is 0.7 us more in stage one, 5.5 less in stage two and 2.6 less in stage three. (Stage one differs by up to 1.4 us between profiles of kernels that are alike in it.) In stage three the sixth product is 1.6 to 2.1; the last `xn` locks (2.4 us of VectorE's time from h) and a shorter low stretch (3.4 us for 7) lie there as well, so these parts are not separate. All three edits have the convolution first too. Against them the changed kernel wins 2.5 us in stage one, the warm-ups' 1.5 included, and 0.6 us of waits in stage two, or 1.6 with the waits that the filler took up. That bounds what TensorE's written order gives there. The token-side LN and the new last attention were not tried alone.

**The convolution.** "3.7 us of convolution no longer lie in stage two" was counted in full as work. It held: stage one is no longer than before, and the work is gone from stage two. In the kernel before the same move gained nothing (1.6 us won in stage two for 3.2 in front), also once GpSimd's order was changed (1.4 for 3.1). So the step would have failed as a general claim; what makes the difference was not tried one by one.

**The rule that spoke against the change.** The row first: the powers of LN1 beside `centre_and_gain` in stage two.

```profile
24.78 0.70 POOL L1756 TENSOR_TENSOR rstd<-mv,minus_half 128x2 f32<-128x2 f32 x1 [3.94 <-DVE mv L929]
...
25.17 0.34 DVE L933 SCALAR_TENSOR_TENSOR xg<-x,mv,norm_rows_sb 128x128 f32<-128x128 f32 x1
...
60.49 0.60 DVE L933 SCALAR_TENSOR_TENSOR xg<-x,mv,norm_rows_sb 128x128 f32<-128x128 f32 x2
```

The power takes 0.70 us at 24.78, and `xg`, which started beside it at 25.17 with two inputs in SBUF, its usual 0.34; at 60.65, with `xg` begun at 60.49, the power takes 0.73 (its row stands above); the one at 50.59 takes 0.71. Only the first, at 19.86, takes 0.97, beside the 128 by 512 `qkw_lo`, and it took 0.98 before [rows 4]. So at most 0.03 us an LN was lost after the first, not 0.3, and the sum without the 1.2 us was the right one. By the rule of the Trainium skill (SBUF — State Buffer, section Who interferes with whom) `xg` would have waited to 25.48; the timeline has it run beside the power, and the measurement decides. For the long pairs the trace agrees with the same section of the Trainium skill: it counts `tensor_scalar` among the forms that can take the shared ports, says that the instruction which comes later waits for the whole of the other, and that one with at most one input in SBUF, outside the modes that use both ports, does not contend. `xn` beside 1.39 us of GpSimd takes 1.67, the `var` of 2 columns takes 0.98 for 0.17, and the sums over q beside the moved weight instructions, which have one input and are not of those forms, keep their 0.68 us.

**Stage three, 51.4; measured 52.0.** The walk held at most of its points, counted from 83.5, the end of that addition: first feed-forward product 4.2 (4.3 forecast), feed-forward done 12.5 (12.5), last LN turned 16.6 (16.3), head done 18.2 (17.6), numerators 31.2 (31.6), last `proj3` 48.7 (49.8), from the last output instruction to the end 2.9. The first rival was there in part: one low stretch of 3.4 us instead of the 14 us it supposed, and it cost about 1 us, by the two profiles whose last stage has none. One gain of this stage the prediction didn't name: [rows 4] show only the `xn` from x, and those from h, which stand in the last stage, had 3.9 us of locks of their own before (6.5 us busy for the 2.7 they take now).

**VectorE as the bound** (0.04) is excluded: 46 us busy in the 60.4 of stage two.

## What to carry to other kernels

Where two engines share ports, read the maximum beside the median of the same instruction: [rows 4] pointed at more than half of this gain by the medians, and the order of one engine brought it without touching the arithmetic. A long GpSimd weight instruction belongs beside VectorE work that was seen to lose nothing (sums, statistics, additions from PSUM), never directly behind the result that VectorE waits for. After moving one, look at what moves up into its place and at every small VectorE instruction beside its new one: list VectorE's busy time by instruction, because the total hides new locks behind old ones that went. Price a wait with the clock that it takes away afterwards, not by its length alone. And before a low clock that went away is put down to an edit, look at the same place in a kernel without the edit.

## What the runs showed of the hardware

- **More waiting goes with more low clock, which can double a wait's price.** Three locks of 3.3 us in all cost 5.5 us by the medians, and TensorE was busy 3.7 us longer with the same instructions; 7.1 us less of locks in the kernel before shortened the profiled span behind the first key product by 10.2.
- **Low stretches also appear where TensorE is busy**, and differ from run to run of one kernel: at 54 to 57 us in the profiles of four edits of the changed kernel and not in its own, although the waits of TensorE ahead of it (0.2 to 0.3 us each, 52 to 54.5) are its own too. The reverse is seen too: after the same waits of 1.75, 0.39 and 0.54 us the clock fell to 0.50 in the changed kernel and stayed at 1.00 in two of its edits without filler. The mean granted clock of a run goes with a part of the spread only: five runs without the warm-ups at 0.975 lie between 137.8 and 140.0 us.
- **With one thin place filled, a low stretch can stand at another** (109 to 116 us in the kernel before with both edits, 54 to 57 in the changed one). That filling can hold the clock up is likely by the three of four filled runs of the kernel before at 1.00, where no unfilled one had more than 0.965. With GpSimd's order changed too, none of six filled runs had more than 0.977, and for the changed kernel it is not shown.
- **The lock is one of form and order**: three-operand `xg` and `y` of 128 columns beside the end of a power lose nothing measurable, `y` beside a long product loses most of it (1.81 us for 0.61, beside 1.47). The size of the VectorE instruction doesn't matter: an addition to 2 columns from SBUF waited as long (0.98 us for 0.17), while sums from SBUF beside long GpSimd work kept their 0.68 us.
